# State-space stage: chunk states in three 16-bit passes behind the x projection, VectorE's state steps in one row

## What is computed

```python
xBC = silu(causal_conv4(hidden @ in_proj_w.T) + conv_b)     # x, B, C
xdt = x * dt
scores = einsum('bclhn,bcshn->bchls', C, B) * Lmat           # Lmat = exp of differences of cs
Ydiag = einsum('bchls,bcshp->bclhp', scores, xdt)
states = einsum('bclhn,bchl,bclhp->bchpn', B, exp(cs_last - cs), xdt)
# scan over chunks: new = carry * exp(cs_last) + states; prev = carry
Yoff = einsum('bclhn,bchpn,bchl->bclhp', C, prev, exp(cs))
y = (Ydiag + Yoff + x * D) * silu(gate)     # then a group norm and the output projection
```

## Time and profile before

| what | us |
|---|---|
| median of 3 runs | 2510.91 |
| lowest and highest run | 2509.49, 2511.23 |
| the profiled execution, its own time | 2510.36 |
| its span, first to last instruction | 2508.4 |
| mean granted TensorE clock | 0.983 of 2.4 GHz |

### The profile page before, as it was taken

The page is one execution under the profiler, slowest core; times in us unless marked ns, Lnnn a source line. Parts: engine busy times, 40 slices in busy tenths (PEclk is TensorE's granted clock), DMA queues, the critical chain, the costliest instruction groups (busy, mean ns, idle before and its releaser), DMA issues. The chain is left out here.

```text
span 2508.4 us, 49070 instructions
## 1 busy us (share of the span) xinstructions
PE 2402.9 (96%) x15624; PEld 1370.3 (55%) x15624; DVE 1816.7 (72%) x3227; ACT 1586.6 (63%) x3317; POOL 1248.7 (50%) x986
## 2 busy tenths in 40 slices
PE   6999999999999999999999998879999999999797
PEld 3555555555555555555555554445555555555343
DVE  4777777777777777777777877577777777788422
ACT  5766766766766766766766765355556566566322
POOL 4455555555556555556556558343433434454123
PEclk8999999999999999999999999889999999999899
DMA  6343343343343343343343341320110110000000
GB/s 237 96 133 114 101 133 114 101 133 114 101 133 114 101 133 114 101 133 114 101 133 114 117 144 61 125 99 1 43 43 1 44 43 12 32 18 1 1 0 34
DMA packets 112867, 218.79 MB, mean 87 GB/s; under 512 B 9440, under 2 KB 42848, under 8 KB 110400
## 3 DMA queue, kind: packets, MB, share of 16 engines
q1 hardware_dynamic: 112576, 215.28, 26.5%
HBM read 212.10 MB, written 3.15 MB: 86 GB/s over the span
## 5 line engine op out<-in xcount | busy, mean ns | idle before, releaser
L1201 POOL TENSOR_TENSOR acc<-acc,sq 128x512 f32<-128x512 f32 x112 | 183.1, 1634 | 274.2 <-ACT sq L920 274.2
L908 ACT ACTIVATE E<-wq,cst 128x128 f32<-128x128 f32 x1024 | 311.6, 389 | 0.3 <-PEq L289 0.3
L255 DVE SCALAR_TENSOR_TENSOR xc<-bank,taps,xc 128x511 f32<-128x511 f32 (+2 forms) x384 | 284.3, 740 | 23.4 <-ACT xc L242 6.4
L1836 POOL TENSOR_TENSOR qT<-qT,qrot 128x512 f32<-128x512 f32 x64 | 81.2, 1269 | 370.9 <-DVE qrot L1733 370.9
L1187 POOL TENSOR_TENSOR ecs<-ecs,xcC 128x768 f32<-128x768 f32 x128 | 261.2, 2040 | 1.8 <-POOLq L289 1.8
L59 PE MATMUL bank<-xhi,wx 128*128 128x512 f16 x640 | 243.4, 380 | 2.9 <-DVE xcB L255 2.9
L1085 DVE SCALAR_TENSOR_TENSOR u<-xc,D,bank 128x512 f32<-128x512 f32 x128 | 95.7, 747 | 204.7 <-PE bank L737 190.7
L61 PE MATMUL bank<-xhi,wx 128*128 128x512 f16 x640 | 243.6, 381 | 0.0
L60 PE MATMUL bank<-xlo,wx 128*128 128x512 f16 x640 | 243.6, 381 | 0.0
L1024 DVE TENSOR_TENSOR E<-E,cbm 128x1024 f32<-128x1024 f32 x128 | 233.5, 1824 | 0.8
L225 POOL TENSOR_TENSOR wolo<-wo 128x512 f16<-128x512 f32 x64 | 69.8, 1091 | 259.5 <-DMA wo<-in_w_o 259.5
(11 more groups left out here) (239 smaller groups left out, 6386.2 us busy)
## 6 DMA issues: line engine op xcount, KB each, us to landing
wq<-cs_rows SPq DMA_DIRECT2D x128, 512.0 KB, 4.2
ecs<-ecs_rows SPq DMA_DIRECT2D x128, 384.0 KB, 3.6
wx<-in_w_xbc SPq DMA_DIRECT2D x80, 256.0 KB, 2.7
wz<-in_w_z SPq DMA_DIRECT2D x64, 256.0 KB, 2.7
wo<-in_w_o SPq DMA_DIRECT2D x64, 256.0 KB, 4.1
wq<-in_wq SPq DMA_DIRECT2D x8, 1024.0 KB, 5.7
awo<-in_wo SPq DMA_DIRECT2D x8, 1024.0 KB, 5.0
wkv<-in_wkv SPq DMA_DIRECT2D x8, 512.0 KB, 3.8
```

What stands on the lines that cost most here:

```text
L255: self.nc.vector.scalar_tensor_tensor(out=dst[:, d:T], in0=self.k.bank[bank][:, 0:T - d], scalar=self.taps[:, bass.ds(g, 1), b, j, 3 - d:4 ...
L908: ins = nc.scalar.activation(E[t.i % 4][:, h, c], sc.csr[t.i % 2][:, h, c * P:(c + 1) * P], ACT.Relu, scale=-1.0, bias=head(sc.cst, t, c, h))
L1201: nc.gpsimd.tensor_tensor(acc[t.b][:], acc[t.b][:], sq[:], ALU.add).then_inc(acc_done, 1)
```

## The change

It does the following.

- `states` uses three 16-bit passes per chunk instead of one 32-bit product: 9 passes instead of 3 products. Its operands are `bthi`, `btlo`, `xwhi`, `xwlo`.
- The tables are scaled so that the decayed x has more room in 16 bits: `wdec` is 16 times larger, and the decays at `ecs` are 16 times smaller (an added bias of the exponential).
- ScalarE gets `leading_x` (xwhi = 16-bit copy of xw) as the first item of each slot, for tile n+1, ahead of the exponentials. GpSimd gets `rest_of_x` (xwlo) as its first item, ahead of `decayed_C`. VectorE gets `rest_of_B` once per unit, after ScalarE's copy of the transposed B, which now makes `bthi`.
- On PE `states` moves from right behind `scan` to behind the x projection, followed by `gate`; `turn_x` comes behind the gate.
- On VectorE the three state steps come together, after `masked`, and `turned_x` moves from ahead of the x taps to behind them.
- `xw` has one buffer instead of two; new waits follow from these.

```diff
...
                 act.wait_ge(v, 4)
                 nc.scalar.activation(t1[:], t1[:], ACT.Ln).then_inc(a, 1)
                 act.wait_ge(v, 9)
-                nc.scalar.activation(ecsT[:], cs[:], ACT.Exp).then_inc(a, 1)
+                act.wait_ge(consts, 5)
+                nc.scalar.activation(ecsT[:], cs[:], ACT.Exp, bias=less[:]).then_inc(a, 1)
                 for c in range(TT):
                     s = slice(c * P, (c + 1) * P)
                     last = nc.scalar.activation(wdecT[:, s], cs[:, s], ACT.Exp, scale=-1.0,
...
                 def evacuate(n):
                     t, j = tables[n]
                     act.wait_ge(tr, n + 1)
-                    nc.scalar.copy((sc.cst, sc.dtt, sc.wdec, sc.cd)[t][:, 4 * j:4 * j + 4].rearrange("p c g h -> p c (g h)"),
-                                   k.bank[4 + n % 4][:, :].rearrange("p (c h) -> p c h", h=P)).then_inc(ev, 1)
+                    nc.scalar.activation((sc.cst, sc.dtt, sc.wdec, sc.cd)[t][:, 4 * j:4 * j + 4].rearrange("p c g h -> p c (g h)"),
+                                         k.bank[4 + n % 4][:, :].rearrange("p (c h) -> p c h", h=P), ACT.Copy,
+                                         scale=X_SCALE if t == 2 else 1.0).then_inc(ev, 1)
 
                 act.wait_ge(loaded, 16 * 5)
                 for q, (tile, bank, dst) in enumerate(first):
...
 
         E = [sb(f"E{i}", [P, 2, CH, P]) for i in range(4)]
         xt = [sb(f"xt{i}", [P, CH, P]) for i in range(2)]
-        xw = [sb(f"xw{i}", [P, CH - 1, P]) for i in range(2)]
+        xw = sb("xw", [P, CH - 1, P])
+        xwhi, xwlo = ([sb(f"xw{n}{i}", [P, CH - 1, P], F16) for i in range(2)] for n in ("hi", "lo"))
         st = [sb(f"st{i}", [P, CH - 1, P]) for i in range(2)]
         u = [sb(f"u{i}", [P, T]) for i in range(2)]
         gz = [sb(f"gz{i}", [P, T]) for i in range(2)]
...
         sq = sb("sq", [P, T])
         acc = [sb(f"acc{i}", [P, T]) for i in range(NB)]
         cbm = [sb(f"cbm{i}", [P, CH, P]) for i in range(NB)]
-        bt = [sb(f"bt{i}", [P, CH - 1, P]) for i in range(NB)]
+        bthi, btlo = ([sb(f"bt{n}{i}", [P, CH - 1, P], F16) for i in range(NB)] for n in ("hi", "lo"))
         ms, rstd = sb("ms", [P, CH]), sb("rstd", [P, CH])
         lin = Linear(k, io, sc, (cbm[0][:].rearrange("p c t -> p (c t)"), acc[0][:]), tmp)
         norms = lin.norms
...
         out_half, cb_ready, bt_ready, ss_ready = S("out_half"), S("cb_ready"), S("bt_ready"), S("ss_ready")
 
         clip_done, exp_done, sq_done, hi_done, gz_done, bt_done = S("clip_done"), S("exp_done"), S("sq_done"), S("hi_done"), S("gz_done"), S("bt_done")
+        xwhi_done, btlo_done, xwlo_done = S("xwhi_done"), S("btlo_done"), S("xwlo_done")
 
         y_done, yg_done, s_step, m_done, xt_done = S("y_done"), S("yg_done"), S("s_step"), S("m_done"), S("xt_done")
...
 
                     pe.wait_ge(m_done, t.n + 1)
                     pe.wait_ge(cs_done, t.n + 1)
+                    pe.wait_ge(s_step, t.n * 3 + 3)
                     pe.wait_ge(gz_done, t.n + 1)
                     for c in range(CH):
                         cols = slice(c * P, (c + 1) * P)
...
                     mm.then_inc(y_ready, 1)
 
                 def states(t):
-                    pe.wait_ge(xw_done, t.n + 1)
-                    pe.wait_ge(bt_done, t.u + 1)
+                    pe.wait_ge(xwlo_done, t.n + 1)
+                    pe.wait_ge(btlo_done, t.u + 1)
+
+                    pe.wait_ge(xt_done, t.n + 1)
                     for c in range(CH - 1):
-                        mm = nc.tensor.matmul(W[:, c * P:(c + 1) * P], bt[t.b][:, c], xw[t.i % 2][:, c], start=True, stop=True)
+                        mm = product(nc, W[:, c * P:(c + 1) * P], (bthi[t.b][:, c], btlo[t.b][:, c]),
+                                     (xwhi[t.i % 2][:, c], xwlo[t.i % 2][:, c]), True, True)
                     mm.then_inc(st_ready, 1)
 
                 def turn_x(g, m):
...
                 def slot(g, m):
                     s = tile_at(g, m)
                     scan(s)
-                    if tile_at(g, m + 1):
-                        states(tile_at(g, m + 1))
                     if s.i == 0 and not (isinstance(s.u, int) and s.u == 0):
-                        pe.wait_ge(bt_done, s.u + 1)
+                        pe.wait_ge(btlo_done, s.u + 1)
                         sum_squares(1 - s.b, s.u, s.n)
                     t = tile_at(g, m + 3)
                     if t:
...
                         sc.project(sc.wx[2 + t.i], t.b, ring_bank(s.b, x_use(s)), sc.xp_ready)
                     if is_last_unit(s):
                         tail(s)
+                    if tile_at(g, m + 1):
+                        states(tile_at(g, m + 1))
+                        gate(tile_at(g, m + 1))
                     if tile_at(g, m + 2):
                         turn_x(g, m + 2)
-                    if tile_at(g, m + 1):
-                        gate(tile_at(g, m + 1))
                     nu = next_unit(s)
                     if nu and s.i == 2:
                         pe.wait_ge(sc.conv_step, 3 * (conv_of_slot(s, "B") - 2) + 3)
...
                     act.wait_ge(z_ready, t.n + 1)
                     nc.scalar.activation(gz[t.i % 2][:], Y[:, :], ACT.Silu).then_inc(gz_done, 1)
 
+                def leading_x(t):
+                    act.wait_ge(xw_done, t.n + 1)
+
+                    wait(act, st_ready, t.n - 1)
+                    nc.scalar.copy(xwhi[t.i % 2][:], xw[:]).then_inc(xwhi_done, 1)
+
                 def turned_B(t, bank):
                     act.wait_ge(bt_ready, t.u + 1)
-                    nc.scalar.copy(bt[t.b][:], k.bank[bank][:, 0:(CH - 1) * P].rearrange("p (c n) -> p c n", n=P)).then_inc(bt_done, 1)
+                    nc.scalar.copy(bthi[t.b][:], k.bank[bank][:, 0:(CH - 1) * P].rearrange("p (c n) -> p c n", n=P)).then_inc(bt_done, 1)
 
                 def first():
                     decays(tile_at(0, 0))
...
                     exps(tile_at(0, 0))
                     gate(tile_at(0, 0))
                     turned_B(tile_at(0, 0), ring_bank(1, USE_BT))
+                    leading_x(tile_at(0, 0))
                     decays(tile_at(0, 2))
 
                 def slot(g, m):
                     s = tile_at(g, m)
+                    if tile_at(g, m + 1):
+                        leading_x(tile_at(g, m + 1))
                     if m % 2 == 0:
                         for d in (1, 2):
                             if tile_at(g, m + d):
...
                     nc.vector.tensor_tensor(by_head(xt[t.i % 2][:]), by_head(W[:, :].rearrange("p (c d) -> p c d", d=P)),
                                             of_heads(sc.dtt, t, 0, CH), ALU.mult).then_inc(xt_done, 1)
 
+                def rest_of_B(t, bank):
+                    dve.wait_ge(bt_done, t.u + 1)
+                    nc.vector.tensor_tensor(btlo[t.b][:], k.bank[bank][:, 0:(CH - 1) * P].rearrange("p (c n) -> p c n", n=P),
+                                            bthi[t.b][:], ALU.subtract).then_inc(btlo_done, 1)
+
                 def masked_CB(t, bank):
                     dve.wait_ge(cb_ready, t.u + 1)
                     nc.vector.tensor_tensor(cbm[t.b][:], k.bank[bank][:, :].rearrange("p (c t) -> p c t", t=P),
...
                     dve.sem_inc(evac_done, 4)
                     turned_x(tile_at(0, 0))
                     masked_CB(tile_at(0, 0), ring_bank(1, USE_CB))
+                    rest_of_B(tile_at(0, 0), ring_bank(1, USE_BT))
                     for c in range(CH - 1):
                         state(tile_at(0, 0), c)
                     masked(tile_at(0, 0))
...
                     dve.wait_ge(y_ready, s.n + 1)
                     nc.vector.scalar_tensor_tensor(out=u[s.i % 2][:], in0=sc.xc[s.i % 4][:], scalar=chan(sc.D, s), in1=Y[:, :],
                                                    op0=ALU.mult, op1=ALU.add).then_inc(y_done, 1)
-                    if n1:
-                        state(n1, 0)
                     dve.wait_ge(y_done, s.n + 1)
                     nc.vector.tensor_tensor(u[s.i % 2][:], u[s.i % 2][:], gz[s.i % 2][:], ALU.mult).then_inc(yg_done, 1)
                     if n1:
-                        state(n1, 1)
-                        state(n1, 2)
                         masked(n1)
                     if ended:
                         mean_square(s.u, s.b)
-                    if n2:
-                        turned_x(n2)
+                    if n1:
+                        for c in range(CH - 1):
+                            state(n1, c)
 
                     def taps(kind, dst, t, j, behind=(None, None)):
                         q = conv_of_slot(s, kind)
...
                         taps("x", sc.xc[n3.i % 4], n3, 2 + n3.i, (remainder, None))
                     else:
                         remainder()
+                    if n2:
+                        turned_x(n2)
                     if nu and s.i == 2:
                         taps("B", sc.xcB, nu, 0)
                     if nu and s.i == 4:
```

(20 more changed lines are left out.)

## The result

| | before | after |
|---|---|---|
| median of 4 runs each, us | 2511.07 (2509.49 to 2512.99) | 2546.01 (2544.65 to 2546.79) |
| ratio to before, 95% interval | | 1.0136 (1.0124 to 1.0148) |
| span of the profiled execution, us | 2508.4 | 2542.0 |
| mean granted TensorE clock | 0.983 | 0.982 |

The account below looks back on a forecast made before the run. TensorE's instruction stream was taken to bound the stage nearly end to end. Eight groups at +3.6 gave +29, less 3 for the last unit, plus about 1.5 for the first state: +27 on 2510.4, thus 2537 us, range 2496 to 2576.

Parts of the forecast that it names:

- TensorE's saving: States on TensorE: nine 16-bit passes take 0.51 us instead of 0.77; 0.2 us saved a slot, bounds 0.16 and 0.26.
- The steady part, +3.6 a group: Each group of slots: -2.8 for 14 slots, plus 2.4, 0.55, 1.6, 0.55 and 1.3, giving +3.6 us.
- The 1.3: Slots 0 and 1 of each group: later residual additions and states behind masked lengthen the pair by 1.3 us (0.1 to 2.3).
- ScalarE's copy push the exponentials: Even slots: late copy delays exponentials, masked and states; 0.5 us stall in 2, 4, 10, 12, 0.2 in 6, 14; 2.4 a group.
- `decayed_C` as a separate term: Slots 3, 5, 11 and 13: decayed_C on GpSimd may hold up VectorE's gate product and masked; 0.4 us each, 1.6 a group.
- The gate's term: ScalarE's gate ends later, about when TensorE's stream does: 0.3 us in slot 6, 0.25 in slot 8, 0.55 a group.
- Slot 9: VectorE starts 0.9 us late, as add_output comes behind a later xt; 0.55 us of it reaches the transposes.
- less 3 for the last unit, which has no B or C: Last unit: 3 us taken off the eight groups' +29 because it has no B or C.
- The signs: Passes 0.057 us apart; copy about 2 us into even slots; transposes wait in 2, 4, 10, 12; scan waits for gate; masked's mean up.
- (1): Rival: the slack holds, stalls only in slots 0 and 1; 2487 us, or 2497 with 0.15 stalls in even slots; chance 0.17.
- (4): Rival: each 16-bit pass costs its weight load's 0.097 us, nine take 0.87; 2576 us; chance 0.03.
- (3): Rival: stalls as forecast or worse, decayed_C ahead of masked everywhere, bubble 0.5; up to 2575 us; chance 0.72 with the forecast.

Follow-up runs that it names:

- run 1: Kernel before with only the new TensorE and VectorE orders; states stay 32-bit, no copy, no rests: 2493.19 us, ratio 0.9938.
- run 5: Changed kernel with decayed_C ahead of rest_of_x on GpSimd, and in the last unit both ahead of the linear layer's work: 2486.05 us, ratio 0.9903.
- run 4: Changed kernel with decayed_C moved behind the squares' sum on GpSimd: 2511.37 us, ratio 1.0007.
- run 7: run 5 plus an idle 768-column ScalarE copy ahead of the exponentials in even slots: 2503.30 us, ratio 0.9969.
- Run 3: Changed kernel with rest_of_x and decayed_C ahead of the linear layer's work in the last eight slots: 2530.67 us, ratio 1.0086.
- run 6: Changed kernel with decayed_C ahead of rest_of_x in every slot, both still behind the linear layer's work in the last unit: 2519.49 us, ratio 1.0033.

## Why the prediction was right, and where its reasons were not

The direction, the range and the size held: 2537 forecast, 2546 measured, 1.36% slower. By its steps:

**TensorE's saving** (0.2 a slot, bounds 0.16 and 0.26): right, at the upper end; 10.75 to 10.50. Runs 1 and 5 split it in 0.09 and 0.16. The 0.1 us that I took for a loss on the way from 32-bit to 16-bit was lost inside the states, right behind the scan, and the new place saved it.

**The steady part, +3.6 a group.** Groups 2 to 7 take 190.4 us on average against 188.1: +2.3. Slots 0 and 1 together are 1.26 longer (I had 1.3), the other fourteen 1.1 (I had 2.3). The 1.3 came out by luck: I had the transposes' wait in slot 1 grow, and it went from 1.21 to 1.04 us a group; what is new is the scan's 1.22 on "issue", for which I had no term. In the fourteen the sign and half the size held, and the form: a stall of the transposes on VectorE's states. Its cause, as I gave it for the even slots, did not. I had ScalarE's copy push the exponentials, these masked, and these the states, 0.5 us each in slots 2, 4, 10 and 12. The copy did begin late, though at 1.2 to 1.4 us instead of 1.9. But in slot 12 of run 4, with ScalarE's chain as late as in the changed kernel and only the neighbour on GpSimd gone, the stall is gone too. In the changed kernel it was mostly `u` times the gate that waited, 1393 ns in the mean instead of 765, and in slot 12 masked. I had `decayed_C` as a separate term, 1.6 a group, for masked in the odd slots; in fact it was nearly the whole. The slots that it hit were only in part those I named: against their length before less 0.25, in the mean of groups 2 to 7 slot 4 lost 1.05, slot 7 0.9, slots 12 and 5 0.65 and 0.6, slot 2 0.45, 6 and 10 0.3 to 0.4, 3 0.2, and 11 and 13 nothing. In these last `decayed_C` begins at 4.1 to 4.3 us, when `u` times the gate is over.

**The gate's term**, 0.55 a group: wrong. The scan waited for the gate once in the whole stage (2.6 us), while run 7 needed 0.83 us more on ScalarE to make it wait 23 times. I had the copy begin at 1.9 instead of some 1.3, and that difference is near the slack. Part of it is a slip of mine: the 3.55 at which I had masked start still holds the copy of state 0, which the change takes from in front of it; in run 1 masked starts at 3.3.

**Slot 9**, 0.55: `u` was 0.4 late and nothing waited for it; it lasted 10.50.

**The first state**, +1.5: measured +0.9.

**The step that failed is "less 3 for the last unit, which has no B or C".** It measured +22.6. I had looked at what the last eight slots lack, and not at what they carry: the linear layer's dequantising on GpSimd, up to 9 us at a stretch (1562.28 to 1571.24 above). It has been harmless, since nothing behind it on GpSimd was wanted before the next scan. The change puts `rest_of_x` there, and TensorE wants it 4.3 us into the slot, ahead of the gate projection and the transposes. That is the very sort of thing that my own price for `rest_of_x` left out: 0.83 us for the operation, nothing for what it queues behind. Run 3 shows it (22.6 became 2.2), and run 6 from the other side.

So the total came out near by luck, because two errors had opposite signs: seven and a half groups at 3.6 would be 27 us and were 15, and the last half group, -1.2 by my sum (its 1.8 less 3), was +22.6. The sum had nothing for the stretch behind the last scan, which was 5 us shorter in the profiles.

**The signs and the rivals.** Of the signs that I had named, the passes' 0.056 and masked's mean (1824 to 1885 ns) came. The transposes' wait came in slots 4 and 12, only faintly in 2 and 10, and also in 5 and 7, which were not among the signs; the scan's wait for the gate did not come. The slack did not hold (1), though it does with one swap of GpSimd's order and the end mended: run 5 at 2486 is what that rival gave, 2487. The weight loads of (4) did not come: nine passes 0.50 us. The number fell inside (3), whose `decayed_C` part is the mechanism that the runs show.

## What to carry to other kernels

Price a new operation not by its duration alone but by what stands ahead of it in its queue, in every stage that has that queue, the last one too, where other work has been put because nobody waited for it. Among an engine's first items, the one that needs nothing new goes ahead of the one that waits for a neighbour; here that swap, with the last unit mended, turned 35 us of loss into 25 of gain. When a moved operation is blamed for a stall, compare the mean time of the operations around it before and after: the one that grew (765 to 1393 ns) is the one that was stopped, and the timeline beside it names the neighbour.

## What the runs showed of the hardware

**VectorE and GpSimd took whole turns.** In slot 4 of the changed kernel `u` times the gate began at 1261.13 and `decayed_C` at 1261.12; the latter ran for 1.82 us, as it does in run 5 too, and the former ended 0.55 us behind it, somewhat less than the 0.68 that it lasts alone. Masked the same: `wolo` ended at 1264.39, masked 1.08 later. I had reckoned masked at half a turn (1.65, between 1.1 and 2.18); none of the rows shown has such a half. The Trainium skill (SBUF — State Buffer, Who interferes with whom) says that a VectorE instruction with two SBUF inputs and a GpSimd one that reads SBUF block each other for a whole instruction; the rows agree. So whether a small operation costs 0.7 or 2.4 us can hang on which of the two engines issues first.

**The same 32-bit products cost less between 16-bit ones than right behind other 32-bit ones.** The states took 0.77 us right behind the scan and 0.67 between the x and the gate projection in run 1; the difference lies between their first and second record. Why is not shown.

**After a long wait the passes came at the lower clock.** The window behind the 8.0 us wait, with the columns of the earlier trace rows:

```profile
1572.00:1576.00 4.00, 3.79 (x16) 2.01 (x17) 2.22 (x6) 0.00 (x0) 3.13 (x3) 0.50 0.00 0
```

The granted clock is 0.50 there, the lower of the two levels (1.2 GHz), after TensorE had idled for 8 us, and the same states' passes start 0.107 us apart (three in 1572.83 - 1572.51) instead of 0.056. The gate projection's passes behind them start 0.42 us apart instead of 0.22. The last unit's loss is thus not its waits alone; how much of it the lower clock made I did not take apart.
